# Row maxima of the attention scores: taken four strips at a time beside the feed-forward part, and one bank at a time beside the attention

## The reference, cut to what matters

```
q, k: 16 sub-heads of 8 features, rotary;  v: 8 heads of 16
probs = softmax(q k^T)                      # 16 x 1024 x 1024 for each of 2 batches
diff  = probs[even] - lam * probs[odd]      # per head
attn  = rms_norm(diff v) * (1 - LAMBDA_INIT) @ Wo^T
ffn   = sum over the 3 best of 8 zones: weight * gelu(xn @ Wa[e]) @ Wb[e]
```

## Time and profile before

| | us |
|---|---|
| median of 3 runs (505.49 to 506.4) | 506.34 |
| the profiled execution | 503.22 |
| its span, first to last instruction | 501.4 |
| PE, DVE, ACT, POOL busy | 443.7, 398.2, 305.1, 62.5 |
| granted clock of PE, mean | 0.971 |

### The profile page before, as it was taken

The page is one execution under the profiler, slowest core; times in us unless marked ns, Lnnn a source line. Parts: engine busy times, 40 slices in busy tenths (PEclk is TensorE's granted clock), DMA queues, the critical chain, the costliest instruction groups (busy, mean ns, idle before and its releaser), DMA issues.

```text
span 501.4 us, 6997 instructions
## 1 busy us (share of the span) xinstructions
PE 443.7 (88%) x2559; PEld 189.9 (38%) x2559; DVE 398.2 (79%) x746; ACT 305.1 (61%) x376; POOL 62.5 (12%) x69
## 2 busy tenths in 40 slices
PE   6496699999899998998999989999899999899985
PEld 5385544444455433332332322333323333222223
DVE  2776689996556788998999999999999989986125
ACT  1441222122123378788877887887888887788972
POOL 8166740100100000000000000000000000000000
PEclk9697799999999999999999999999999999999997
DMA  8207873110000000020020020020020000000002
GB/s 304 103 8 247 251 255 132 44 43 1 1 2 1 0 3 1 3 75 1 1 76 1 3 75 1 3 73 3 2 75 1 3 0 3 1 3 3 0 2 84
DMA packets 11796, 23.62 MB, mean 47 GB/s; under 512 B 1498, under 2 KB 6234, under 8 KB 11634
## 3 DMA queue, kind: packets, MB, share of 16 engines
q1 hardware_dynamic: 11330, 20.37, 13.1%
q10 hardware_dynamic: 432, 2.81, 1.5%
HBM read 14.43 MB, written 8.39 MB: 46 GB/s over the span
## 4 chain that ended last, share of the span: by engine, by line
PE 54%; DVE 20%; ACT 9%; issue 9%; DMA 4%; SPq 2%; POOL 1%; ACTq 0%; DVEq 0%; POOLq 0%
PE ps L986 15%; PE ps L955 15%; DVE part_max L678 15%; PE ps L911 9%; ACT E L514 8%; PE ps L979 5%; DMA X<-in_x 2%; PE ps L829 2%; PE ps L830 2%; PE ps L831 2%; DMA q_scr<-ropeL 1%; SPq L298 1%; ACT A L533 1%; PE ps L944 1%; DVE zT L783 1%
## 5 line engine op out<-in xcount | busy, mean ns | idle before, releaser
L678 DVE TENSOR_REDUCE part_max<-ps 128x1 f32<-128x512 f32 x512 | 321.4, 682 | 47.2 <-PE ps L955 43.2
L514 ACT ACTIVATE E<-ps 128x1024 f32<-128x1024 f32 x256 | 244.3, 1027 | 52.8 <-PE ps L979 52.5
L955 PE MATMUL ps<-K,Q 32*128 32x512 f32 x512 | 162.1, 462 | 14.7 <-DVE part_max L678 13.5
L986 PE MATMUL ps<-E,Vg 128*32 128x512 f32 x1024 | 136.4, 605 | 1.7 <-ACT E L514 1.0
L955 PEld LDWEIGHTS ps<-K,Q 32*128 32x128 f32 x512 | 70.3, 182 | 149.0 <-DVE part_max L678 137.4
L979 PE MATMUL ps<-Q,K 32*128 32x512 f32 x512 | 111.6, 467 | 12.5 <-ACT E L514 11.7
L493 ACT ACTIVATE h<-ps 128x512 f32<-128x512 f32 x48 | 28.7, 597 | 86.7 <-PE ps L831 86.7
L979 PEld LDWEIGHTS ps<-Q,K 32*128 32x128 f32 x512 | 44.4, 182 | 42.2 <-ACT E L514 39.3
L911 PE MATMUL ps<-h,wb_f 128*128 128x512 f32 x96 | 51.9, 624 | 0.0
L436 POOL TENSOR_TENSOR U<-AT,rsum 128x256 f32<-128x256 f32 x15 | 9.3, 620 | 320.6 <-DVE rsum L750 320.6
L829 PE MATMUL ps<-xnH,waH 128*128 128x512 f32 x48 | 36.2, 754 | 0.0
(11 more groups left out here) (133 smaller groups left out, 266.6 us busy)
## 6 DMA issues: line engine op xcount, KB each, us to landing
Q<-q_scr SPq DMA_DIRECT2D x8, 512.0 KB
K<-k_scr SPq DMA_DIRECT2D x32, 96.0 KB
tab<-in_tables ACTq DMA_DIRECT2D x1, 2048.0 KB, 10.8
q_scr<-ropeL SPq DMA_DIRECT2D x4, 512.0 KB, 5.8
q_scr<-ropeH SPq DMA_DIRECT2D x4, 512.0 KB, 6.7
k_scr<-ropeH SPq DMA_DIRECT2D x4, 512.0 KB, 5.0
wa_raw<-in_wa SPq DMA_DIRECT2D x6, 256.0 KB, 2.7
wb_raw<-in_wb SPq DMA_DIRECT2D x6, 256.0 KB, 2.9
```

The costliest lines, as they stand in the source:

```text
L514: nc.scalar.activation(E[:, par, 2 * jj:2 * jj + 2, :].rearrange("p j t -> p (j t)"), ps[:, 2 * jj:2 * jj + 2, :].rearrange("p j t -> p (j ...
L678: nc.vector.tensor_reduce(part_max[:, half, col, sh:sh + 1], ps[:, SLOT_BANK[unit_slot(2 * q) + 2 * sh + u], :], AX.X, ALU.max).then_inc(s ...
L955: mm(ps[:, SLOT_BANK[x], :], Q[rows, g % KQ_BUFS, k // GJ * P:(k // GJ + 1) * P], K[rows, g % KQ_BUFS, j % 2, sh * BANK:(sh + 1) * BANK], ...
L986: last = mm(ps[QUAD * j:QUAD * (j + 1), B_PV, :], Vg[:, par, st, j // 2, :], E[:, s % 2, k, :], start=(st == 0), stop=(st == TB - 1), skip ...
```

## The change

- A "quad" t takes the place of the pair: one tile, one half of the keys, all four strips. The steps of the feed-forward part with maxima are now n with n % 4 < 3, 36 steps, from n = 0. Ring there: 4, 5, 2, 3 below n = 22; 4, 5, 3, 0 for n = 22 to 25; 4, 5, 0, 1 after.
- In the attention part the 368 slots that are left go singly: 3 or 4 in a step (20 steps have 4), over the same 116 steps. On PE a step is now four scores, all slots, products.
- K is compact: one plane for each buffer, 128 rows, one DMA of 512 KB. Its rows of ones come from a filled DRAM buffer (two more DMAs of 512 KB at the start; 12 small DMAs and the clearing of K go). The first K and Q load is issued ahead of the last four reads of the picked zones.
- `back`, the residual on DVE and what waits for them go. The tail adds the feed-forward sums by four more products for each chunk. The chunks' sums start one by one, at n = 24 and n = 28.
- SP's list: `max_rows` 3 ahead of the fourth group's load, 4 alone with it, then two for each load.

```diff
-LEAD_STEPS = tuple(range(3, 22)) + (22, 24, 26, 28) + tuple(range(30, 47, 2))
+LEAD_STEPS = tuple(n for n in range(UNITS) if n % 4 < 3)
...
+def quad_slot(t):
+    return 4 * t + max(0, (t - 1) // 8)
...
-    return (4, 5, 2, 3) if n < 22 else (4, 5) if n < 30 else (4, 5, 0, 1)
+    return (4, 5, 2, 3) if n < 22 else (4, 5, 3, 0) if n < 26 else (4, 5, 0, 1)
...
-def half_pairs(s):
-    return 2 * LEAD + min(2 * (ALL_PAIRS - LEAD), -(-(s + 1) * 2 * (ALL_PAIRS - LEAD) // MAX_STEPS))
+def max_slots(s):
+    def up_to(n):
+        return 4 * LEAD + min(4 * (QUADS - LEAD), -(-n * 4 * (QUADS - LEAD) // MAX_STEPS))
+    return [divmod(x, 4) for x in range(up_to(s), up_to(s + 1))]
...
-("K", [P, KQ_BUFS, 2, SEQ], F32R)
+("K", [P, KQ_BUFS, SEQ], F32R)
...
             def kq_load(i):
-                for j in range(GJ):
-                    sp.dma_start(K[QUAD * j:QUAD * j + PROD_ROWS, i % KQ_BUFS, j % 2, :].bitcast(F32),
-                                 k_scr[i, j]).then_inc(kq_in[i % KQ_BUFS], 16)
+                sp.dma_start(K[:, i % KQ_BUFS, :].bitcast(F32), k_scr[i]).then_inc(kq_in[i % KQ_BUFS], 16)
...
-            for hx in range(1, 3):
+            for hx in range(1, 4):
                 max_rows(hx)
-            for i, halves in zip(range(KQ_BUFS, GROUPS), ((3, 4), (5, 6), (7,), (8, 9), (10,))):
+            for i, halves in zip(range(KQ_BUFS, GROUPS), ((4,), (5, 6), (7, 8), (9, 10), (11, 12))):
...
+            def reduce_slot(t, k):
+                tile, sh, j = t // 2, t % 2, PLACE[k]
+                dve.wait_ge(slot_made[j], t + 1)
...
+                if k < GJ - 1:
+                    return
+                if t % TB == TB - 1:
...
+                if t % TB == 0 and t:
+                    max_split(t // TB - 1)
...
+            def max_slot(t, k):
+                tile, sh, j = t // 2, t % 2, PLACE[k]
+                g, x = tile // TB, quad_slot(t) + k
+                if tile % TB == 0 and sh == 0 and k == 0:
+                    pe.wait_ge(kq_in[g % KQ_BUFS], 32 * (g // KQ_BUFS + 1))
+                ring_free(x)
+                mm(ps[:, SLOT_BANK[x], :], Q[strip(j), g % KQ_BUFS, tile % TB * P:(tile % TB + 1) * P],
+                   K[strip(j), g % KQ_BUFS, sh * BANK:(sh + 1) * BANK], start=True, stop=True).then_inc(slot_made[j], 1)
+                if k == GJ - 1 and t % TB == 0 and t:
+                    half_transpose(t // TB - 1)
...
             for s in range(ALL_STEPS):
                 nxt = s + 1
-                made = [(hp // 2, hp % 2) for hp in range(half_pairs(s - 1), half_pairs(s))]
-                if made:
-                    pair_slot(*made[0], 0)
+                made = max_slots(s)
                 if nxt < ALL_STEPS:
...
                     pe.wait_ge(exp_done, 2 * s + 1)
+                    score(nxt, 0)
                     score(nxt, 1)
-                    score(nxt, 0)
-                if made:
-                    pair_slot(*made[0], 1)
-                if nxt < ALL_STEPS:
                     pe.wait_ge(exp_done, 2 * s + 2)
                     score(nxt, 2)
                     score(nxt, 3)
-                for q, sh in made[1:]:
-                    for u in range(2):
-                        pair_slot(q, sh, u)
+                for t, k in made:
+                    max_slot(t, k)
...
             def residual(c):
-                mm(ps[:, O_BANK[c], :], ident, RES[:, c * FC:(c + 1) * FC, :].rearrange("p n d -> p (n d)"),
+                mm(ps[:, O_BANK[c], :], ident, X[:, c * FC:(c + 1) * FC, :].rearrange("p n d -> p (n d)"),
                    start=True, stop=False, skip_group_check=True)
+                for k in range(FC):
+                    mm(ps[:, O_BANK[c], k * P:(k + 1) * P], zT[:, (c * FC + k) * P:(c * FC + k + 1) * P], ident,
+                       start=False, stop=False, skip_group_check=True)
...
-            for c in range(2):
-                residual(c)
+            residual(0)
             heads_sum(3)
+            residual(1)
             residual(2)
```

More of the change, by code:

```diff
@@ L111, with last_lead_slot @@
 assert len(SLOT_BANK) == SLOTS
-def last_lead_slot(banks):
-    return max(x for x in range(unit_slot(2 * LEAD)) if SLOT_BANK[x] in banks)
-def half_pairs(s):
-    return 2 * LEAD + min(2 * (ALL_PAIRS - LEAD), -(-(s + 1) * 2 * (ALL_PAIRS - LEAD) // MAX_STEPS))
+def last_lead_slot(banks, steps=UNITS):
+    quads = sum(n < steps for n in LEAD_STEPS)
+    return max(x for x in range(quad_slot(quads)) if SLOT_BANK[x] in banks)
+def max_slots(s):
+    def up_to(n):
+        return 4 * LEAD + min(4 * (QUADS - LEAD), -(-n * 4 * (QUADS - LEAD) // MAX_STEPS))
+    return [divmod(x, 4) for x in range(up_to(s), up_to(s + 1))]
 HEADS_AT = (MAX_STEPS + 2, MAX_STEPS + 3, ALL_STEPS - 3)
@@ L276, in _, with fill_rows @@
                 sp.dma_start(dst[:], src).then_inc(s_in, 16)
+            def fill_rows(scr, part):
+                for half in range(2):
+                    sp.dma_start(scr[half * GB:(half + 1) * GB].rearrange("g (j s r) t -> (g j) s r t", j=GJ, r=DQ)[:, 3],
+                                 part[:, 1, :].bitcast(F32)).then_inc(fill_out, 16)
             sp.wait_ge(fills2, 1)
[L279 to L287, removed]
+            fill_rows(q_scr, ropeL)
+            sp.wait_ge(fills2, 2)
+            fill_rows(k_scr, ropeH)
             def scratch(n):
@@ L364, in _ @@
                 kq_load(i)
-            for hx in range(11, 2 * GROUPS):
+            for hx in range(13, 2 * GROUPS):
                 max_rows(hx)
@@ L922, in _ @@
             first(2)
-            def back(c):
-                pe.wait_ge(z_out, c + 1)
-                for k in range(FC):
-                    last = nc.tensor.transpose(ps[:, back_bank(c), k * P:(k + 1) * P],
-                                               zT[:, (c * FC + k) * P:(c * FC + k + 1) * P], ident)
-                last.then_inc(zt_done, 1)
             def ring_free(x):
@@ L990, in _ @@
             for n in range(UNITS):
-                if n == UZ * TOP_K:
-                    pe.wait_ge(slot_read, last_lead_slot((2, 3)) + 1)
-                    start_sums(1)
+                for c in range(CB, CHUNKS):
+                    if n == UZ * TOP_K + (c - CB) * FC:
+                        pe.wait_ge(slot_read, last_lead_slot((c,)) + 1)
+                        start_sum(c)
                 a = n + H_LEAD
@@ L1002, in _ @@
                 if n in LEAD_STEPS:
[L1003 to L1007 removed]
+                    for k in range(GJ):
+                        max_slot(LEAD_STEPS.index(n), k)
                 if n % UZ == 0:
@@ L1011, in _ @@
                 second(n)
-                for c in range(CHUNKS - 1):
-                    if n == sum_steps(c) + 2:
-                        back(c)
             pe.wait_ge(qmax_in, 32)
```

161 lines of the change are left out of this document (56 added, 105 removed).

## The result

The changed kernel is slower: 518.4 us in the median of its executions against 506.3 for the kernel before, a ratio of 1.023 with a 95% interval of 1.018 to 1.027. (A ratio here leaves out executions more than 1.5% above the fastest of their kernel; a median does not.) The forecast was 506.6 with a range of 501.5 to 511.5, so it is wrong by 12 us. The profiled execution took 514.5 us (span 512.7) against 503.2 (501.4), 11.3 longer.

What follows compares the result with a forecast made beforehand. It took the hand-over between DVE and PE as the bound. Feed-forward -0.8, 116 steps -0.8, load +2.7 and tail -0.8 made +0.3 on the profiled 503.22: 503.5, or 506.6 in the median, range 501.5 to 511.5.

Steps and rivals of the forecast that it cites:

- Feed-forward part: Up to step 0's product with V: four more quads done in the same time; -0.8 us after correction.
- 116 steps: Attention part, steps 0 to 116: 280.8 us less a correction of 1.5, against 280.1 before; -0.8.
- The load: Fourth group's K and Q load lands late, so PE, DVE and ACT stand in step 15; +2.7 us.
- rival D: Fourth group's load lands in time, all else as in the sum: 503.9 us; chance 0.07.
- Tail: End of the kernel: last eight products in 1.2 us, PE never idle before them; -0.8 us.
- the two corrections that were taken off: Stepping rules' excess on the order of before: 0.8 us up to step 0's product, 1.5 over the 116 steps.
- Rival C: Attention part: maxima behind both exponential waits leave DVE a gap in every three-slot step; 509 to 518 us, chance 0.21.
- rival B: Attention part: singly placed slots keep DVE fed, down to its lower bound, -14 us; 493 to 504, chance 0.22.
- Early quads: Feed-forward part: four more quads done in the same time, nothing gained on the clock.

Runs made afterwards that it cites:

- e6: Changed kernel with both the order of a step as in the kernel before and a fourth K/Q buffer: 486.0 us, ratio 0.962 to before.
- e1: Changed kernel with a fourth K/Q buffer, the fourth group loaded during the feed-forward part: 510.7 us, ratio 1.010 to before.
- e8: Kernel before with one added wait of TensorE in step 14, for two fills on GpSimd: 512.8 us, ratio 1.008 to before.
- e2: Changed kernel with the order of a step as in the kernel before, otherwise unchanged: 494.0 us, ratio 0.975 to before.
- e4: Changed kernel with a 128x512 product of zero weights ahead of the third slot in 7 of 8 steps: 557.1 us, ratio 1.096 to before.
- e7: e1 with only the first slot of a step moved ahead of the exponential waits: 490.2 us, ratio 0.969 to before.
- e9: e6 with the kernel before's 32 early steps, leaving 384 slots instead of 368: 482.7 us, ratio 0.954 to before.
- e3: Changed kernel with the kernel before's 32 early steps, leaving 384 slots instead of 368: 511.3 us, ratio 1.014 to before.
- e13: e1 with a 128x256 product of zero weights ahead of the third slot, 7 of 8 steps from step 9: 525.2 us, ratio 1.036 to before.
- e5: Kernel before with only the order of a step changed to the new one (four scores, then all maxima): 599.1 us, ratio 1.182 to before.

## Why the prediction was wrong

- **Feed-forward part: arithmetic right, clock missed.** Measured blocks of 2.18, 3.07, and 3.97 for the last two, ten of them in 96.0. Step 0 is at 181.6 instead of 179.1. The low stretches at 66.5 and 172.3 stand where about 1.6 of this was lost: the quad of n = 4 is 0.9 late, and from that of n = 44 to step 0's product it is 13.0 instead of 12.4. Another 0.8 was taken off the sum for the error of the rules, and that did not show.
- **116 steps at full clock: right, the pattern only in part.** Forecast (280.8 - 1.5) / 116 = 2.408 a step, measured 2.430 in clear ones. Three-slot steps take 2.17 (forecast 2.12), four-slot steps 3.14 (2.95), those with a half transpose 3.33 (3.4). But 1.79 and 2.43 do not take turns: 27 of the 74 plain three-slot steps are the short ones, in sequences like 1.79, 2.43, 2.48.
- **The load: right.** TensorE's gap of 2.80 ends by a DMA in step 15; the step is 2.6 over a clear one (forecast 2.7), so rival D is out.
- **Tail: right in kind.** -0.5 instead of -0.8, and no low clock in the products.
- **The step that failed** is a term that is not in the sum: I read "granted clock of 1.00" in the earlier trace rows and carried it over to an order in which TensorE waits in other places. No line of the sum prices time at the lower level, in the attention part or ahead of it. The profiled execution of after is 11.0 us over its forecast of 503.5. It pays 5.8 for low stretches in the attention part and about 1.6 ahead of it, two thirds of the miss; 2.3 are the two corrections that were taken off (0.8 and 1.5); the rest, 1.3, are small errors of the terms. In the medians the miss is 11.8, since after gains 0.8 more time over its profiled execution than before does.
- **What is shown of the cause, and what is not.** e6 and e1 differ only in the order, and the trace of one has no low stretch from step 0 to 116 and the other three; over all executions the granted clock is 0.961 to 0.971 in e6 and 0.950 to 0.958 in e1. So the order brings them. That a gap brings one is borne out by e8 and by the load's gaps of after, e2 and e4, four of four. That it is the shorter waits of the new order that bring the others is not shown, nor which length or kind of wait would do it.
- **Rival C** has the time that came out, 518, but not its mechanism: three-slot steps above 2.4 as a rule would have been its mark, and 27 of 74 take 1.79 or little more. That the number fits is luck. Still its subject was the important one. The order does cost 0.17 us a step against the old order on the same slots, 24 us with its low stretches (e2, e6, e7). My sum didn't show it, since the other parts of the change give about as much in the 116 steps: 18.0 by e6 (262.1 against 280.1, past **rival B**'s bound of 266.5), 9.2 of them for the 16 slots that are no longer there and 8.8 for the rest (e9), in which the single slots were not tested by themselves. I stepped the new slots in the new order only, and so saw two large terms as one near zero.
- **Early quads:** forecast neutral. In the new order they are (e3), in the old one they cost 3.3 us (e9). Here too a zero hid two terms: with before's early steps the feed-forward part is 10 to 11 us shorter (step 0 at 170.0 in e3 and 168.7 in e9), and four more quads take all of it.

The Trainium skill (TensorE: Matmul & The Clock Gate, "A second HAM failure mode: psum-queue depth-cycling") tells of a kernel whose small waits between groups of matmuls, as it goes round PSUM's banks, are enough to make the clock go to and fro between its two levels. The clock of after does go to and fro on a ring of three banks (eight low stretches), and that of e6 doesn't between step 0 and 116 on the same ring; that the small waits do it is not shown here. Had I weighed that passage, it would have been a rival with the right sign.

What is open: what brings the low stretches without a gap, and what ends one. In after they last 3.4 us, behind or in a single gap 13.7 (e8) and 17.1 (e2), and 31 and 41 with TensorE never idle (e13, e4).

## What to carry to other kernels

When a change moves an order and changes the pieces in it, step each alone against the same partner: two terms of nearly 20 us can make a zero, and then the half that costs can be put back (here one slot ahead of the waits, 20 us). Put work that another engine is waiting for, and that is free to go, ahead of any wait in an in-order queue, not behind it. A granted clock of 1.00 holds for the order, and the execution, in which it was read; where a change gives TensorE a gap of 2 us or more, price a stretch behind it, in these traces half of TensorE's speed for 3 to 41 us.

## What the runs showed of the hardware that was not expected

- Gaps of 2.21 (e8), 2.53 (e4) and 2.80 us (after) on TensorE were each followed by a stretch at the lower clock level, 13.7, 41.0 and 3.4 us long; in e2 one of 17.1 began inside a gap of 3.82. A gap of 1.91 in the tail, the same in three kernels, was followed by one in the kernel before and in e8, and not in the 6 us up to the end in e5. The steps in low stretches take 0.22 to 0.40 us more per us of it than clear ones (excess over low, in the table, where low is above 10).
- TensorE busy without any idle time at the lower level stayed there for 41.0 us (e4) and 30.7 us (e13). A fuller TensorE did not bring the clock back sooner: the two kernels with the filler have the longest stretches.
- A full product of 512 columns added where TensorE often waited for a read, in 7 of 8 steps, made a clear step 0.20 us longer; one of 256 columns 0.14 us. The wait was not slack: what stands behind it came later.
- Executions of one program differ most where its traces show gaps or many low stretches: by 9.8 us in e8 (509.3 to 519.1) and 12.9 in e5 (596.9 to 609.8), against 1.5 in e9 (482.2 to 483.7).
